# Attention heads leave the tensor engine untransposed: transfers pack them, and one scaled product per half feeds the output projection

## The reference

```python
x = x + jnp.tanh(g_xattn[0]) * _L0_xattn_ref(_layernorm(x), ctx_1024, ctx_1024, adj, mask, Wq, bq, ...)
x = x + jnp.tanh(g_ffn[0]) * _L0_ffn_ref(_layernorm(x), gate_w, w1, b1, w2, b2)
...
    scores = jnp.einsum('bhqd,bhkd->bhqk', Q, K) / jnp.sqrt(jnp.float32(D))
    scores = scores + adj[None, None, :, :]
    scores = jnp.where(mask == 0, jnp.float32(-jnp.inf), scores)
    weights = jax.nn.softmax(scores, axis=-1)
    out = jnp.einsum('bhqk,bhkd->bhqd', weights, V)
    out = out.transpose(0, 2, 1, 3).reshape(b, s, E)
    return jnp.einsum('bse,ef->bsf', out, Wo.T) + bo
...
    for e in range(n_experts):
        ye = jax.nn.relu(x @ w1[e] + b1[e]) @ w2[e] + b2[e]
        sel = (expert_idx == e)[:, None]
        out = out + jnp.where(sel, ye * expert_w[:, None], 0.0)
```

## Time and profile before

| | |
|---|---|
| three runs | 551.56, 551.67, 552.55 us; median 551.67 |
| profiled execution | span 548.5 us from its first to its last instruction; no separate time is listed for it, so what lies around the span is taken as 551.67 - 548.5 = 3.2 us |
| TensorE busy | 526.3 us, 96% |
| VectorE, ScalarE, GpSimd busy | 302.3, 309.1, 297.9 us |
| transfers | 77.67 MB, 142 GB/s on average |

### The profile page before, as it was taken

The page is one execution under the profiler, slowest core; times in us unless marked ns, Lnnn a source line. Parts: engine busy times, 40 slices in busy tenths (PEclk is TensorE's granted clock), DMA queues, the critical chain, the costliest instruction groups (busy, mean ns, idle before and its releaser), DMA issues. The chain is left out here.

```text
span 548.5 us, 13306 instructions
## 1 busy us (share of the span) xinstructions
PE 526.3 (96%) x4123; PEld 405.1 (74%) x4124; DVE 302.3 (55%) x923; ACT 309.1 (56%) x678; POOL 297.9 (54%) x424
## 2 busy tenths in 40 slices
PE   8999999989999999999999999888999999999997
PEld 5577667667666667666676666658899999999996
DVE  2776587976677887668885878845340211111111
ACT  4366678665678665778675676664332333333322
POOL 5346566665567575468574556555244444443451
PEclk9999999999999999999999999999999999999999
DMA  8633625400405510204520057499136665555570
GB/s 288 206 110 132 192 65 183 149 31 6 150 21 192 166 50 1 79 10 153 180 85 1 11 184 250 147 362 320 59 103 218 211 205 196 178 187 184 189 210 1
DMA packets 51489, 77.67 MB, mean 142 GB/s; under 512 B 9945, under 2 KB 34601, under 8 KB 51305
## 3 DMA queue, kind: packets, MB, share of 16 engines
q1 hardware_dynamic: 46600, 67.72, 37.0%
q0 software_dynamic: 4192, 8.73, 5.0%
q10 hardware_dynamic: 640, 0.52, 0.3%
HBM read 52.76 MB, written 8.35 MB: 111 GB/s over the span
## 5 line engine op out<-in xcount | busy, mean ns | idle before, releaser
L1588 DVE CUSTOM_DVE_ANT_0 prob<-bank,adjm 128x512 f32<-128x512 f32 x256 | 172.3, 688 | 70.6 <-issue 39.9
L1229 ACT ACTIVATE pt<-bank 128x512 f32<-128x512 f32 x256 | 152.1, 596 | 87.7 <-PE bank L951 81.2
L682 POOL TENSOR_SCALAR prob<-prob,negmax 128x512 f32<-128x512 f32 x190 | 132.0, 698 | 117.6 <-DVE negmax L1588 113.4
L951 PE MATMUL bank<-ident,prob 128*128 128x128 f32 x1024 | 154.8, 274 | 2.2 <-POOL prob L682 1.3
L951 PEld LDWEIGHTS bank<-ident,prob 128*128 128x128 f32 x1024 | 124.2, 141 | 39.7 <-issue 13.7
L1299 ACT ACTIVATE adjm<-bank,colsm 128x128 f32<-128x128 f32 x184 | 52.6, 368 | 105.0 <-PE bank L1127 80.0
L940 PE MATMUL bank<-w2s 128*128 128x512 bf16 x256 | 97.5, 381 | 8.5 <-DVE negmax L1588 5.7
L963 PE MATMUL bank<-pt,vals 128*32 128x256 f32 x1024 | 68.3, 385 | 0.9 <-DVE vals L1386 0.5
L1127 PEld LDWEIGHTS bank<-xT,pt 128*128 128x128 f32 x576 | 67.1, 192 | 0.9
L1127 PE MATMUL bank<-xT,pt 128*128 128x128 f32 x576 | 67.2, 275 | 0.0
L1137 PE MATMUL bank<-w2s,adjm 128*128 x288 | 65.1, 379 | 0.0
(11 more groups left out here) (195 smaller groups left out, 624.4 us busy)
## 6 DMA issues: line engine op xcount, KB each, us to landing
pt<-in_L_ffn_w SPq DMA_DIRECT2D x19, 1024.0 KB
w2s<-parts SPq DMA_DIRECT2D x96, 128.0 KB
w2s<-in_L_ffn_w SPq DMA_DIRECT2D x8, 1024.0 KB
maski<-in_mask_Bx1xSxS_ik SPq DMA_DIRECT2D x4, 1024.0 KB, 5.6
w2s<-parts SPq DMA_DIRECT2D x56, 64.0 KB, 2.1
xres<-in_x SPq DMA_DIRECT2D x18, 128.0 KB
x_d<-rows SPq DMA_DIRECT2D x18, 128.0 KB
xn_d<-rows SPq DMA_DIRECT2D x18, 128.0 KB
```

The lines of the kernel that those rows point to most:

```text
L682: po.tensor_scalar(prob[:, m], prob[:, m], -1.0, negmax[:, m:m + 1], ALU.mult, ALU.add).then_inc(s_shpool, 1)
L951: mm = pe.transpose(tr_bank[n % NTB][:, c * P:(c + 1) * P], prob[:, n % TILES % NB, c * P:(c + 1) * P], ident[:])
L1229: act.activation(pt[:, g % 2, :, j, q2 * P:(q2 + 1) * P], tr_bank[c % NTB][:].rearrange("p (c q) -> p c q", c=QT), ACT.Exp).then_inc(s_cac ...
L1588: ve.tensor_tensor_reduce(out=prob[:, m % NB], in0=sc_bank[m % NS][:], in1=adjm[:, qt], scale=-1.0, scalar=BIG, op0=ALU.add, op1=ALU.min, ...
```

## The change

Heads are no longer transposed and transposed back, except in the tail of the very last half. `o_sb` already has the channels on partitions, with gaps. SP now issues copies within SBUF: `compact` (eight transfers of 32 KB for a half, four after each pair of groups) closes the gaps into `oc`, one more transfer of 16 KB gathers the 16 rows of sums into `rc` (16 partitions x 256, a part of the tile `rest`); VectorE inverts `rc` in place (`invert`); SP issues four transfers of 64 KB that `spread` each inverse over its head's 16 partitions into `rs`; VectorE multiplies `oc` by `rs` into `atT` (`scale`, 128 x 512); and `out` takes `atT` as it is. A half has one `invert` and one `scale`, at steps 14 and 20 and at 47 and 52 (46 and 50 in the last round). The first round also has its `invert` at step 14, on the ones that `o_sb` was filled with. ScalarE's copy to `o_sb` gets waits on the transfers that read it, two halves back. ScalarE's copies behind `turn` go too. Some steps of the tables move by one or two.

```diff
@@ -100,18 +100,14 @@
     PRE = len(PRO)
     FIRST_NEXT = PRO.index("next x")
     NEXT = 8
-    TAIL_A = [(15, "heads", 0), (18, "heads", 1), (23, "turn", 0), (25, "turn", 1), (29, "out", 0),
-              (33, "out", 1), (38, "normed", 0), (41, "normed", 1), (44, "gate", (0, 1)), (51, "rank", 0)]
+    TAIL_A = [(29, "out", 0), (33, "out", 1), (38, "normed", 0), (41, "normed", 1), (44, "gate", (0, 1)), (51, "rank", 0)]
     USES = sorted([(10, "values", 0), (11, "values", 1)] + TAIL_A
                   + [(12, "next x", 0), (14, "next x", 1), (17, "next ctx", 0), (19, "next ctx", 1),
                      (20, "next q", 0), (26, "next k", 0), (30, "next q", 1), (35, "next k", 1)]
-                  + [(45, "heads", 2), (46, "heads", 3), (50, "turn", 2), (52, "turn", 3), (53, "out", 2),
-                     (56, "out", 3), (61, "normed", 2), (63, "gate", (2,)), (65, "normed", 3),
+                  + [(54, "out", 2), (57, "out", 3), (62, "normed", 2), (64, "gate", (2,)), (65, "normed", 3),
                      (68, "gate", (3,))], key=lambda use: use[0])
-    LAST_USES = sorted([(10, "values", 0), (11, "values", 1), (13, "heads", 0), (14, "heads", 1), (16, "turn", 0),
-                        (18, "turn", 1), (20, "out", 0), (22, "out", 1), (27, "normed", 0), (29, "normed", 1),
-                        (31, "gate", (0, 1)), (39, "rank", 0), (45, "heads", 2), (46, "heads", 3), (48, "turn", 2),
-                        (50, "turn", 3), (52, "out", 2), (55, "out", 3), (60, "normed", 2), (62, "gate", (2,)),
+    LAST_USES = sorted([(10, "values", 0), (11, "values", 1), (22, "out", 0), (24, "out", 1), (29, "normed", 0), (31, "normed", 1),
+                        (33, "gate", (0, 1)), (41, "rank", 0), (52, "out", 2), (55, "out", 3), (60, "normed", 2), (62, "gate", (2,)),
                         (65, "normed", 3), (67, "gate", (3,))], key=lambda use: use[0])
     LAST_TAIL = [("heads", 0), ("heads", 1), ("rank", 0), ("turn", 0), ("turn", 1), ("out", 0), ("out", 1),
@@ -122,15 +118,16 @@
 
     ACT_AT, VE_AT, ACT_QK_AT, VE_QK_AT = 1, 1, 2, 3
     OUT_STATS_AT = VE_AT + 1
-    OUT_RSTD = ({32: 0, 36: 1, 56: 2, 59: 3}, {23: 0, 25: 1, 55: 2, 59: 3})
-    ROW_STEPS = ({36: 0, 39: 1, 59: 2, 63: 3}, {25: 0, 27: 1, 57: 2, 61: 3})
-    SHIFT_STEP, EXP_STEP, PICK_STEPS = (45, 33), (46, 34), ((47, 48, 49), (35, 36, 37))
+    SUMS_STEPS, SCALE_STEPS = ((14, 47), (14, 46)), ((20, 52), (20, 50))
+    OUT_RSTD = ({32: 0, 36: 1, 57: 2, 60: 3}, {25: 0, 27: 1, 55: 2, 59: 3})
+    ROW_STEPS = ({36: 0, 39: 1, 60: 2, 63: 3}, {27: 0, 29: 1, 57: 2, 61: 3})
+    SHIFT_STEP, EXP_STEP, PICK_STEPS = (45, 35), (46, 36), ((47, 48, 49), (37, 38, 39))
     STATS_STEPS, RSTD_STEP, NORM_STEPS = (61, 62, 64, 65), 67, (69, 70, 72, 73)
     CAST_STEPS = {n + VE_QK_AT + 1: (i, w, a) for i, (n, w, a) in enumerate(USES)
                   if w in ("next q", "next k")}
     SPLIT_STEPS = {n + 1: use for n, use in CAST_STEPS.items()}
-    SLOT_STEPS, SCATTERED_STEP = ((54, 59, 62, 67), (41, 43, 46, 47)), (73, 60)
-    TABLE_STEPS = (41, 42, 43, 44, 45, 48, 49, 50, 51, 52, 65, 66)
+    SLOT_STEPS, SCATTERED_STEP = ((54, 59, 62, 67), (43, 45, 48, 49)), (73, 60)
+    TABLE_STEPS = (43, 44, 45, 46, 47, 49, 50, 51, 52, 53, 65, 66)
     INDEX_STEP, NORMED_STEPS = TILES - 5, (TILES - 5, TILES - 2)
     ABS_STEPS = {29: 0, 34: 1, 40: 2, 45: 3}
...
         xres = sb("xres", [P, 2, E])
-        attn = sb("attn", [P, 2, E])
-        atT = sb("atT", [P, 2, EC, P])
+        oc = sb("oc", [P, EC, HALF])
+        rc = rest[0:H, 0:HALF]
+        rs = sb("rs", [P, EC, HALF])
+        atT = sb("atT", [P, EC, HALF])
         x2T = sb("x2T", [P, 2, EC, P])
 
-        zrow = atT[0:1, 0].rearrange("p c q -> p (c q)")
-        gate_r = attn[0:X, 0]
+        attn = oc
+        zrow = atT[0:1, 0]
+        gate_r = oc[0:X, 0]
         b2b = maski[:].rearrange("p t s -> p (t s)").bitcast(F32).rearrange("p (x e) -> p x e", x=X)
         hT = adjm[:].rearrange("p t s -> p (t s)").rearrange("p (u c t) -> p u c t", u=2, c=FC)
         xgT = xT[:].rearrange("p k (u t) -> p u k t", u=4)[:, 0:2]
...
@@ -338,6 +338,8 @@
             eng.sem_inc(s_waited[eng is nc.vector], 1)
 
         FIRST = 16 * 2 * PAIRS
+        COMPACT = 16 * 2 * HG
+        SPREAD = 16 * NG
         STACKED = NQ * FIRST
 
         def place_of(h):
@@ -415,6 +417,38 @@
                 sp.dma_start(x1_d[ds((t + u) * P, P), :], rows[:, u, 0:E]).then_inc(t_out[u], 16)
                 sp.dma_start(xn_d[ds((t + u) * P, P), :], rows[:, u, E:2 * E]).then_inc(t_out[u], 16)
 
+            def compact(par, qh):
+
+                for j in range(HG):
+                    to = slice(par * P // 2 + j * D, par * P // 2 + (j + 1) * D)
+                    sp.dma_start(oc[to], o_sb[j * VW:j * VW + D, par::2, qh]).then_inc(t_comp, 16)
+                if par == 1:
+                    sp.dma_start(rc, o_sb[D:P:VW, :, qh]).then_inc(t_sums, 16)
+
+            def spread(b, half):
+
+                sp.wait_ge(t_rc, b * 2 + (half + 1))
+                for a in range(NG):
+                    at = a % 2 * P // 2
+                    sp.dma_start(rs[at:at + P // 2, a // 2], rc[a:H:NG].rearrange("j (o q) -> j o q", o=1).to_broadcast(
+                        [HG, D, HALF])).then_inc(t_over, 16)
+
+            def compact_old(b, par):
+
+                sp.wait_ge(s_osb, b * GROUPS + (2 if par == 1 or b == 0 else 0))
+                if par == 0 and b > 0:
+                    sp.wait_ge(t_atT, b * 2)
+                compact(par, 1)
+
+            def compact_new(b, par):
+
+                sp.wait_ge(s_osb, b * GROUPS + (NG + 1 + par))
+                if par == 0:
+                    sp.wait_ge(t_atT, b * 2 + 1)
+                if par == 1 and b + 1 < B:
+                    sp.wait_ge(s_parts, (b + 1) * 4 + 4)
+                compact(par, 0)
+
             def next_xres(b, nxt, k):
 
                 sp.wait_ge(t_x1, b * 4 + k + 1)
@@ -450,29 +484,44 @@
             for b in range(B - 1):
                 t, par = b * QT, ds((b + 1) % 2, 1)
 
+                if b == 0:
+                    compact_old(0, 0)
+                compact_old(b, 1)
                 sp.wait_ge(s_adjm, b * QT + QT)
                 sp.dma_start(maski[:], m_v[ds(b + 1, 1)].rearrange("b p t e -> p (b t) e")).then_inc(s_mask, 16)
+                spread(b, 0)
                 if b + 2 < B:
                     load_x(b + 2)
                     load_ctx(b + 2)
                 for u in range(2):
                     next_xres(b, t, u)
+                compact_new(b, 0)
                 for u in range(2):
                     rows_out(b, (t + (NT - 2)) % NT, u)
                     sp.wait_ge(s_parts, (b + 1) * 4 + 3)
                     stack_in(sp, par, 0, u, 0, EC, range(PAIRS), s_stack)
                 rows_free(b, 0)
+                compact_new(b, 1)
+                spread(b, 1)
                 sp.wait_ge(s_parts, (b + 1) * 4 + 4)
                 for g in range(NQ):
                     stack_in(sp, par, 1, g, 0, EC, range(PAIRS), s_stack)
-                tail_pair(b, t, 2, t + 2)
+                for u in range(2):
+                    next_xres(b, t + 2, 2 + u)
+                compact_old(b + 1, 0)
+                for u in range(2):
+                    rows_out(b, t, 2 + u)
+                rows_free(b, 2)
 
             def load_w2(e):
                 sp.dma_start(w2s[:, e], w2[e].rearrange("(c p) f -> p c f", p=P)).then_inc(r_w2, 16)
 
 
             last = B - 1
+            compact_old(last, 1)
+            spread(last, 0)
             tail_pair(last, last * QT - 2, 0, last * QT)
+            compact_new(last, 0)
             sp.wait_ge(s_score, last * TILES)
             for e in range(X // 2):
                 load_w2(e)
@@ -487,6 +536,8 @@
                 sp.dma_start(ew1[u], w1_v[ds(e, 1)].rearrange("x p k f -> p (x k) f")).then_inc(e_w1[u], 16)
 
             sp.wait_ge(s_stack, last * STACKED)
+            compact_new(last, 1)
+            spread(last, 1)
             sp.wait_ge(e_eid, 1)
             sp.wait_ge(s_xT, B * 4)
...
                 if what == "out":
-                    pe.wait_ge(t_atT, b * 4 + k + 1)
+                    pe.wait_ge(t_atT, b * 2 + (k // 2 + 1 if b < B else k + 1))
                     o = bank_free(b, i)
                     for c in range(EC):
-                        mm = pe.matmul(o[:, 0:E], atT[:, u, c], wT[:, 3, c], start=c == 0, stop=c == EC - 1)
+                        mm = pe.matmul(o[:, 0:E], atT[:, c, u * P:(u + 1) * P], wT[:, 3, c], start=c == 0, stop=c == EC - 1)
                 if what == "normed":
                     pe.wait_ge(t_row, b * 4 + k + 1)
@@ -1232,6 +1284,9 @@
                 if n >= LO + TPG and (n - LO) % TPG == 0:
                     g = (n - LO) // TPG - 1
                     act.wait_ge(s_pv, b * GROUPS + g + 1)
+                    if b > 0 or g >= NG:
+                        act.wait_ge(t_comp, COMPACT * (b * 2 + g // NG))
```

(16 more changed lines are left out.)

38 lines of the change are left out of this document (21 added, 17 removed).

## The result

The changed kernel takes 613.30 us (median of 4 runs, 612.74 to 615.62), the kernel before on the same chip 552.11 (551.56 to 552.65): a ratio of 1.11, 95% interval 1.1067 to 1.1133. It is slower, as predicted, but outside the range. The profiled execution spans 611.0 us, 62.5 more than before.

What follows compares the result with a forecast made beforehand. TensorE was taken to set the pace, stopped by VectorE's waits on SyncE's list; 18.5 + 1.9 + 7.0 + 2 x 4.6 + 3.8 + 0.5 = 40.9 us on a 548.5 us span, forecast 592 us, range 571 to 603.

Steps and rivals of the forecast that it cites:

- What bounds the kernel: In the rounds TensorE sets the pace; holding VectorE over about 2 us stops it; SyncE's list decides whether waits are met.
- What VectorE gains: VectorE's added work per round: inverses of 2.0 us and `scale` of 0.85, together 5.7 us for 2.7 removed.
- Terms A and B: First round: A, step 14's `invert` waits for late sums, +18.5 us; B, late spread less removed heads and turns, +1.9.
- Term C in round one: Step 47's `invert` waits for sums behind SyncE's stack copies; +7.0 us, as SyncE's run is slower there.
- Term B's sentence on the spread: First round: spread behind the 1 MB mask load waits within the same slow stretch; alone it would cost about 1 us.
- Term C in rounds two and three: Step 47's `invert` waits 5 us for sums behind stack copies; +4.6 us a round, including 1.8 for slow clock.
- Term D: Last round: second-half sums land late behind four 1 MB loads and `b2b`, holding the inverse; +3.8 us.
- Behind the rounds: After the four rounds: the early expert's loads start a step later, +0.5 us.
- The gain: TensorE in four rounds: 24 transposes removed per round give at most 10.4 us, an upper bound.
- the rival of hidden waits: Sums always there when VectorE comes, so removed transposes count: about 541 to 547 us; 3 in 100.

Runs made afterwards that it cites:

- e2: Changed kernel with `spread(b, 0)` issued ahead of the mask load in SyncE's list: 595.31 us, ratio 1.0845.
- e8: Changed kernel with useless products on TensorE ahead of the scores that wait for VectorE in rounds one to three: 612.06 us, ratio 1.108.
- e4: Changed kernel with two of four w2 loads and b2b moved behind `spread(last, 1)`, instead of ahead of the last round's second compacting: 604.90 us, ratio 1.1021.
- mended versions: Versions of the changed kernel with the four single edits together, and further reorderings built on that: the first measured 560.04 us, ratio 1.0129.
- e16: e15 with the last two w2 loads and b2b behind the slots loads, and the second inverse of rounds one to three at step 46: 557.15 us, ratio 1.0078.
- e17: e16 with all four w2 loads and b2b right behind `spread(last, 0)`, ahead of `tail_pair`: 551.60 us against 552.58, ratio 0.9975.
- e7: Kernel before with the heads' and turned transposes of the four rounds issued twice (96 more): 558.81 us, ratio 1.0127.
- four single edits: Changed kernel, each alone: round one's first half dropped; spread before mask load; second sums before eight stack copies; w2/b2b loads later: 586.55, 595.31, 593.54, 604.90 us.
- e9: Changed kernel with the four single edits, gathering before compacting, last round's second inverse a step earlier and first projection a step later: 559.73 us, ratio 1.0169.
- e12: e9 with `spread(b, 1)` straight behind the second sums and their compacting, ahead of the last eight stack copies: 558.62 us, ratio 1.0082.
- e15: e12 with `compact_new(b, 0)` ahead of the second `next_xres`, in idle time of SyncE: 558.36 us, ratio 1.009.

## Why the prediction failed, by its own steps

The time came out 21 us above the sum and 10 above the range. In the terms of the sum, the first round was right in total, rounds two and three lost 22.9 us instead of 9.2, the last 8.8 instead of 3.8, and the stretch behind the rounds 3.7 instead of 0.5.

**What bounds the kernel** was right: whatever holds VectorE stops TensorE, and SyncE's list decides when VectorE is held. Each single edit to that list moved the ledger where it was made and the time by 23.6, 14.8, 16.6 and 5.2 us, within 3 us of the ledger.

**What VectorE gains** was right in direction and close: the inverse takes 1.74 us for the 2.0 of the line through two small ones, `scale` 0.71 for 0.85. The estimate from the repeat count of 8 in the Trainium skill, "VectorE: DVE Perf Modes", section "First, the fixed hardware budget", was 2 us or slightly more; the trace is below that.

**Terms A and B**, 20.4, measured 20.1 at 1:45, by luck. A was 18.5 and measured 16.2 (TensorE's score of step 18 at 66.24 instead of 50.04): SyncE was through with its copies and loads 1.9 us earlier than in before, so the sums were issued at 61.94 for a predicted 63.7, and the inverse was shorter. B was 1.9 and measured 3.9, all of it the late spread by e2, which stands at 16.2 at 1:27. The 2.7 us for the slow clock, less the removed products, do not show: from step 17 to 27 e2 stays within 0.4 us. The clock itself stood at 0.50 from 53.9 to 71.0 us, 4.7 us beyond TensorE's restart. The prediction's 5.4 us for its rise in the prologue were taken from the products' durations; the profile's granted clock of that stretch reads 1.00.

**Term C in round one**, 7.0, measured 6.9 (1:45 to 1:63).

**Term B's sentence on the spread**, "that wait falls into the same slow stretch; it would cost about 1 us alone", and Term C's 0.3 for `scale` at step 20 in ordinary rounds, is the step that failed first. VectorE waited 7.8 and 6.6 us there in rounds two and three. Two things were missing. SyncE cannot issue the mask load before GpSimd has used the mask, and `spread` stands behind that wait: in all three rounds it was issued 3.2 us after the inverse had ended. And behind the 1 MB load the transfers landed 6.4, 6.7 and 5.4 us after their last issue, against 3.7 in the last round, where no mask load stands before them. The row of 5.8 us for a small transfer behind loads was used in Term D for this and not here. e2 takes both away and prices them together: 3.9, 6.4 and 4.1 us in the three rounds, 14.4 in all, as 14.8 measured.

**Term C in rounds two and three**, 4.6 each, is the second. From step 45 to 63 these rounds lose 8.7 and 7.5. VectorE idled 8.2 and 7.0 us, not 5. Set against the masks, which are 31.6 us later than before at 2:45, the sums of round two are issued 4.0 us later than booked. Of this 1.0 is the gain that was taken off and had by then been lost to `scale`. Another 1.5 is the start of the last eight stack copies, behind the four packing copies of `compact_new(b, 0)`, which the prediction did not count. The other 1.5 is that the eight copies took 6.7 us up to the next issue instead of 5.2; why they did is open. The slow clock behind this wait, booked at 1.8 a round, is 1.1 and 0.8 by e8. The one behind the wait for `scale` was not booked: without the filling, rounds two and three lose 2.1 and 0.9 us more from 63 to 27.

**Term D**, 3.8, measured 10.7 from 4:45 to the end of the rounds, less 1.9 gained before it: 8.8. The w2 and b2b loads were issued until 387.6, the sums at 390.2, behind four packing copies, and they landed at 396.3, 6.1 us after. e4, with two of the four loads and b2b out of the way, gives 7.1 of it back by step 51.

**Behind the rounds**, 0.5, measured 3.7. This is not settled in the changed kernel. In the mended versions the same stretch grew by 5 to 10 us, and e16 and e17 put a part of it on slots and w2 that come late.

**The gain** of the removed products, at most 10.4, is 5.6 by e7's ledger. The bound was not passed, and the rival of hidden waits, 541 to 547 us, was not reached by any order of the list that was tried: the best is 551.6.

## What to carry to other kernels

A transfer that a computing engine waits for is priced at its place in the issuing queue, with every issue ahead of it counted (here 0.6 to 0.7 us for most copies of 16 to 128 KB, at times 0.8, and 1.5 to 1.8 us for each 1 MB load when four follow each other). To this come every wait that stands ahead of it in that queue (here one for GpSimd, 3.2 us) and every large load issued just before it. A mechanism found at one place must be asked at all places of the same kind. When a mend moves such a wait and the time stays, look for the next link of the same chain (gather, inverse, spread, product) and for what the mend pushed back. Here it took the four single edits and five further versions (e9, e12, e15, e16, e17) until the whole was ahead of before, one late entry is left, and the gain was a quarter of a per cent. A ledger of one repeated instruction against the kernel before shows where each microsecond goes, also when losses further on hide a gain, or when a sum of zero hides two effects, as in e8.

## What the runs showed of the hardware

An inverse over 256 elements of each of 16 partitions takes 1.74 us, over 16 elements 0.235: 6.3 ns an element. Five DMA issues on ScalarE kept it from computing for 3.8 us. TensorE idled for 17 us in the changed kernel, and its granted clock stayed at 0.50 for 4.7 us after it had restarted. Kept at full clock in rounds two and three by products of no use, the kernel (e8) lost 5 us less there, of 22.9: most of the loss was the waits themselves.
